# Two 16-head attentions: softmax sums written spread over the channels and inverted 512 wide, the spreading products removed, the key projection moved to the query's PSUM bank

## The reference

```python
q = (query @ Wq + bq).reshape(B, Nq, H, D).transpose(0, 2, 1, 3)      # H = 16 heads of D = 16
k = (key_value @ Wk + bk).reshape(B, Nkv, H, D).transpose(0, 2, 1, 3)
v = (key_value @ Wv + bv).reshape(B, Nkv, H, D).transpose(0, 2, 1, 3)
attn = jnp.einsum('bqhd,bhkd->bhqk', q, k) * scale
attn = jnp.clip(attn, -CLAMP, CLAMP)
attn = jax.nn.softmax(attn, axis=-1)
x = jnp.einsum('bhqk,bhkd->bqhd', attn, v).reshape(B, Nq, Cq)
return x @ Wo + bo
```

## Time and profile before

| | |
|---|---|
| median of 3 runs | 5029.59 us (5027.15 to 5030.32) |
| the profiled execution | 5077.9 us, span 5076.2 us |
| busy in the span | PE 4603.2 us (91%), DVE 3162.8 us (62%), ACT 1994.3 us (39%), POOL 1814.7 us (36%) |
| a0, first to last reciprocal | 70.3 to 597.4 us |
| a2, first to last reciprocal | 2164.4 to 2682.5 us |

### The profile page before, as it was taken

How to read it: one execution, slowest core, us unless ns; L and a number is a source line. 1 busy time by engine, 2 the same in 40 slices (tenths; PEclk the granted TensorE clock), 3 DMA queues, 4 the chain that set the end, 5 groups by cost and what they waited for, 6 DMA issues and landing times. The chain is left out here.

```text
span 5076.2 us, 91866 instructions
## 1 busy us (share of the span) xinstructions
PE 4603.2 (91%) x32540; PEld 3590.0 (71%) x32540; DVE 3162.8 (62%) x9688; ACT 1994.3 (39%) x4150; POOL 1814.7 (36%) x2248
## 2 busy tenths in 40 slices
PE   7999689988996999699996999999999967999979
PEld 5666457777775888566665888888888844777856
DVE  6888699965553331277773777777777743444344
ACT  3555367743442332245442333333333322222234
POOL 2222145532453331344530233333333312555532
PEclk9999899988997999799998999999999979999989
DMA  4666412144313222222212111111100055222233
GB/s 117 150 158 150 121 51 70 60 150 133 51 55 66 70 69 69 60 72 65 70 45 76 30 31 31 31 31 30 31 31 29 22 172 174 90 89 92 77 103 109
DMA packets 329713, 397.17 MB, mean 78 GB/s; under 512 B 66021, under 2 KB 289994, under 8 KB 318506
## 3 DMA queue, kind: packets, MB, share of 16 engines
q1 hardware_dynamic: 315946, 366.04, 25.5%
q0 software_dynamic: 13312, 25.25, 2.1%
HBM read 297.64 MB, written 93.55 MB: 77 GB/s over the span
## 5 line engine op out<-in xcount | busy, mean ns | idle before, releaser
L2540 PE MATMUL fa_h<-fa_xnT,fa_w 128*128 128x256 f32 x2048 | 485.6, 383 | 0.0
L2552 PE MATMUL fa_y<-fa_w,fa_hT 128*128 128x256 f32 x2048 | 462.5, 379 | 0.0
L2540 PEld LDWEIGHTS fa_h<-fa_xnT,fa_w 128*128 128x128 f32 x2048 | 382.5, 191 | 71.2 <-issue 13.2
L2552 PEld LDWEIGHTS fa_y<-fa_w,fa_hT 128*128 128x128 f32 x2048 | 386.8, 190 | 65.0 <-issue 14.8
L2419 ACT ACTIVATE fa_hT<-fa_h,fa_b 128x256 f32<-128x256 f32 x512 | 215.0, 471 | 544.2 <-PE fa_h L2540 482.3
L425 DVE TENSOR_REDUCE a_mx<-a_score 128x16 f32<-128x1920 f32 x128 | 275.9, 2156 | 83.8 <-PE a_score L609 74.6
L2926 ACT ACTIVATE m_hT<-m_h,m_b 128x256 f32<-128x256 f32 x256 | 107.5, 471 | 403.8 <-PE m_h L2963 403.8
L1566 PE MATMUL r_h<-r_xnT,r_rw 128*128 128x256 f32 x1024 | 251.2, 395 | 12.4 <-ACT r_hT L1524 11.5
L1867 ACT ACTIVATE e_hT<-e_h,e_b 128x256 f32<-128x256 f32 x256 | 107.5, 471 | 335.6 <-PE e_h L1921 327.6
L1706 POOL DMA_INDIRECT e_xg<-moe_rows,e_idx x64 | 128.6, 2009 | 308.5 <-issue 262.4
L1921 PE MATMUL e_h<-e_xT,e_w 128*128 128x256 f32 x1024 | 234.2, 382 | 2.5 <-DVE e_xT L1720 2.5
(11 more groups left out here) (453 smaller groups left out, 11009.6 us busy)
## 6 DMA issues: line engine op xcount, KB each, us to landing
a_floor<-a_lowest SPq DMA_DIRECT2D x64, 960.0 KB, 6.8
cv_toep<-kernels SPq DMA_DIRECT2D x16, 2048.0 KB
x<-a_xo SPq DMA_DIRECT2D x96, 256.0 KB, 4.1
f_xb<-x SPq DMA_DIRECT2D x64, 256.0 KB, 3.0
f_xres<-x SPq DMA_DIRECT2D x64, 256.0 KB, 3.0
a_xb<-x SPq DMA_DIRECT2D x64, 256.0 KB, 2.8
e_w<-in_L_ffn_ew SPq DMA_DIRECT2D x16, 1024.0 KB, 7.6
a_cb<-in_ctx SPq DMA_DIRECT2D x96, 90.0 KB, 2.3
```

Of the source, the lines that this page charges most:

```text
L2540: last = pe.matmul(h_ps[j % 2][:, c, :], w1[:, e, k, f:f + P], xnT[it.p][:, k, :], start=k == 0, stop=k == KD - 1)
L2552: last = pe.matmul(bank[:, t * D:(t + 1) * D], hT[e % 2][:, k, t * P:(t + 1) * P], w2[:, e, k, :], start=k == 0, stop=k == KE - 1)
```

## The change

`onesel` becomes two matrices of 32 columns, one for the even and one for the odd heads, with ones in 16 adjacent columns; a sum thus comes out of the same number of products on all 16 channels of its head. The two halves `m` no longer accumulate into one block of 256 columns, each has its own, so `total` is full with 512 columns. `reciprocals` becomes `invert`, 512 columns wide, and `weigh` becomes `divide`, which multiplies `raw` by `rec` itself; on DVE `divide` stands directly behind `invert`, ahead of `clips(0)` or `combine`. `widen`, its semaphore and `spread` are gone. `project_k` has no room in `total` any more: it goes to the right half of `front`, which it may write only when `q_out` has read the query from it (`q_ready`), and it stands behind `scores(1)`; `k_out` waits for `project_v` as well, and in a0 stands behind `exps(0)`.

```diff
-            def reciprocals(it):
+            def invert(it):
                 dve.wait_ge(av_ps, KD * it.i + 2)
-                if it.reused(1):
-                    dve.wait_ge(wide_ps, it.i)
-                dve.reciprocal(rec[:], total[:, 0:S]).then_inc(rec_ready, 1)
-
-            def weigh(it):
-                dve.wait_ge(wide_ps, it.i + 1)
+                dve.reciprocal(rec[:], by_k(total[:])).then_inc(rec_ready, 1)
+
+            def divide(it):
+                dve.wait_ge(rec_ready, it.i + 1)
                 dve.wait_ge(raw_ready, it.i + 1)
                 if it.reused():
                     dve.wait_ge(y_ps, it.i - 1)
-                dve.tensor_tensor(oT[it.p][:], raw[:], by_k(back[:]), ALU.mult).then_inc(oT_ready, 1)
+                dve.tensor_tensor(oT[it.p][:], raw[:], rec[:], ALU.mult).then_inc(oT_ready, 1)
...
-                    (3, maxima(0)), (5, reciprocals), (4, clips(0)), (1, norm_stats), (3, maxima(1)), (1, norm), (5, weigh),
+                    (3, maxima(0)), (5, invert), (5, divide), (4, clips(0)), (1, norm_stats), (3, maxima(1)), (1, norm),
...
             def k_out(it):
                 act.wait_ge(k_ps, it.i + 1)
+                act.wait_ge(v_ps, it.i + 1)
...
             def project_k(it):
                 pe.wait_ge(c_in[it.at], 16 * (it.round + 1))
-                if it.reused(1):
-                    pe.wait_ge(k_ready, 2 * it.i)
-                if it.reused(3):
-                    pe.wait_ge(rec_ready, it.i - 2)
+                pe.wait_ge(q_ready, it.i + 1)
                 for m in range(KD):
                     for k in range(2):
-                        last = pe.matmul(total[:, S + m * SK:S + (m + 1) * SK], wk[:, k, m * P:(m + 1) * P], cb[it.at][:, k, :],
+                        last = pe.matmul(front[:, S + m * SK:S + (m + 1) * SK], wk[:, k, m * P:(m + 1) * P], cb[it.at][:, k, :],
                                          start=k == 0, stop=k == 1)
...
                         for g in range(G):
-                            last = pe.matmul(total[g * 32:(g + 1) * 32, 0:S], onesel[:, m * E + e, :], pT[m][:, g, h * S:(h + 1) * S],
-                                             start=m == 0 and h == 0, stop=m == KD - 1 and h == E - 1)
+                            last = pe.matmul(total[g * 32:(g + 1) * 32, m * S:(m + 1) * S], onesel[:, e, :], pT[m][:, g, h * S:(h + 1) * S],
+                                             start=h == 0, stop=h == E - 1)
                     last.then_inc(av_ps, 1)
                 return step
-
-            def widen(it):
-                pe.wait_ge(rec_ready, it.i + 1)
-                if it.reused(1):
-                    pe.wait_ge(y_ready, it.i)
-                for m in range(KD):
-                    last = pe.matmul(back[:, m * S:(m + 1) * S], spread[:, m, :], rec[:], start=True, stop=True)
-                last.then_inc(wide_ps, 1)
```

More of the change, by code:

```diff
@@ L256, in heads_attention @@
                             "v_ready", "kd_ready"))
-    s_ps, maxed, mT_ps, taken, st_ps, exp_ready, av_ps, raw_ready, rec_ready, wide_ps, oT_ready, y_ps, y_ready = (
-        st.sem(n) for n in ("s_ps", "maxed", "mT_ps", "taken", "st_ps", "exp_ready", "av_ps", "raw_ready", "rec_ready",
-                            "wide_ps", "oT_ready", "y_ps", "y_ready"))
+    s_ps, maxed, mT_ps, taken, st_ps, exp_ready, av_ps, raw_ready, rec_ready, oT_ready, y_ps, y_ready = (
+        st.sem(n) for n in ("s_ps", "maxed", "mT_ps", "taken", "st_ps", "exp_ready", "av_ps", "raw_ready", "rec_ready", "oT_ready",
+                             "y_ps", "y_ready"))
     res_ready, bias_in, bias_ps, bias_ready = (st.sem(n) for n in ("res_ready", "bias_in", "bias_ps", "bias_ready"))
     NW = 8
-    MADE = 1 + 4 + 4 + SETS + KD + (1 if clip else 0)
+    MADE = 1 + 4 + 4 + E + (1 if clip else 0)
     MASKS = 9
@@ L320, in _ @@
             pool.wait_ge(made, 9)
-            one4 = onesel[:].rearrange("p j (a r) -> p j a r", r=SETS)
-            for j in range(SETS):
-                pool.memset(one4[:, j, :, j], 1.0).then_inc(made, 1)
-            for m in range(KD):
[L325 to L328, removed]
+            for e in range(E):
+                pool.memset(onesel[:, e, e * DH:(e + 1) * DH], 1.0).then_inc(made, 1)
             if clip:
@@ L472, in _ @@
                 pipeline(dve, B, DEPTH, [
-                    (3, maxima(0)), (5, reciprocals), (4, clips(0)), (1, norm_stats), (3, maxima(1)), (1, norm), (5, weigh),
+                    (3, maxima(0)), (5, invert), (5, divide), (4, clips(0)), (1, norm_stats), (3, maxima(1)), (1, norm),
                     (4, clips(1)), (3, put_max), (5, y_out)], **RUN)
             else:
-                pipeline(dve, B, DEPTH, later([(4, put_max), (3, maxima(0)), (5, reciprocals)]) + ([(2, combine)] if routed else []) + later([
-                    (1, norm_stats), (3, maxima(1)), (5, weigh), (1, norm), (5, y_out)]), **RUN)
+                pipeline(dve, B, DEPTH, later([(4, put_max), (3, maxima(0)), (5, invert), (5, divide)]) + ([(2, combine)] if routed else []) + later([
+                    (1, norm_stats), (3, maxima(1)), (1, norm), (5, y_out)]), **RUN)
         @block.scalar
@@ L506, in k_out @@
                 for m in range(KD):
[L507 removed]
+                    act.activation(kT[it.p][:, m, :], front[:, S + m * SK:S + (m + 1) * SK], ACT.Identity,
                                    bias=bk[:, m:m + 1]).then_inc(k_ready, 1)
@@ L544, in _ @@
                 pipeline(act, B, DEPTH, [
-                    (2, xT_out), (5, raw_out), (2, q_out), (2, k_out), (4, exps(0)), (2, v_out), (3, low_out), (4, exps(1))], **RUN)
+                    (2, xT_out), (5, raw_out), (2, q_out), (4, exps(0)), (2, k_out), (2, v_out), (3, low_out), (4, exps(1))], **RUN)
             else:
@@ L684, in _ @@
                 pipeline(pe, B, DEPTH, [
-                    (2, turn_x), (3, scores(0)), (5, attend(0)), (5, attend(1)), (4, shifted_scores(0)), (2, project_q), (2, project_k),
-                    (3, scores(1)), (5, widen), (2, project_v), (3, turn_max), (4, shifted_scores(1)), (5, project_o)], **RUN)
+                    (2, turn_x), (3, scores(0)), (5, attend(0)), (5, attend(1)), (4, shifted_scores(0)), (2, project_q),
+                    (3, scores(1)), (2, project_k), (2, project_v), (3, turn_max), (4, shifted_scores(1)), (5, project_o)], **RUN)
             else:
                 pipeline(pe, B, DEPTH, later([
-                    (2, turn_x), (3, scores(0)), (5, attend(0)), (5, attend(1)), (4, shifted_scores(0)), (2, project_q), (2, project_k),
-                    (3, scores(1)), (5, widen), (2, project_v), (4, shifted_scores(1)), (5, project_o), (3, turn_max)]), **RUN)
+                    (2, turn_x), (3, scores(0)), (5, attend(0)), (5, attend(1)), (4, shifted_scores(0)), (2, project_q),
+                    (3, scores(1)), (2, project_k), (2, project_v), (4, shifted_scores(1)), (5, project_o), (3, turn_max)]), **RUN)
     st.end()
```

13 lines of the change are left out of this document (6 added, 7 removed).

## The result

The changed kernel takes 5300.42 us (median of 4 runs, 5296.01 to 5303.56), the kernel before 5028.37 us in the same rounds: ratio 1.0539, 95% interval 1.0524 to 1.0554. It is 272 us slower where 161 were forecast. The direction held; the size lies outside the range of 5150 to 5250.

The account below looks back on a forecast made before the run. Neither PE nor DVE fills its stage; a ring of waits, mostly DVE's, sets the pace. Rings 128 us plus a0's clock 33 us make 161 us: 5190.6 us, 3.2% slower, range 5150 to 5250 us.

Parts of the forecast that it names:

- The rings: DVE's closed chain of waits per slot: longer by 2.32 us in a0, 1.95 us in a2; 70 and 58 us.
- The rival with the clock up: PE's clock stays at full speed, leaving only the 128 us of DVE terms: 5158 us, chance 0.22.
- The clock: PE's clock falls in a0 after 3.35 us idle before `scores(1)`: 1.1 us per slot, 33 us.
- I expect no fall there: In a2 the new PE gaps are shorter, so no clock fall; if it falls, 51 us.
- the sum: Whole kernel: 128 us of DVE terms plus 33 us of clock, 161 us, giving 5190.6 us.
- my upper bound of 2.9: Highest clock price per a0 slot, if `turn_max` and `shifted_scores(1)` double and projections outgrow `maxima(1)`: about 2.9 us.
- The rival "clock falls in both": PE's clock falls in a0 and a2, adding 51 us: 5242 us, chance 0.20.
- The key projection: Moved behind `scores(1)`: no change in a0; in a2 it waits for `q_out`, and `y_out` is just not held up.
- POOL's chain: In a2, POOL's work behind `k_out` up to `xres` ends at 11.8 us, before `y_out` at 12.19 us.
- the 48.3 us: Profiled execution of the kernel before stands this far above the median 5029.6 us; the difference carries over.
- the increment in a2: From the reciprocal, `maxima(1)` can start at 6.88 in place of 4.93 us: +1.95 us per slot.
- the slot of 19.05 us: Predicted length of a slot of a2 after the change, named among the signs to look for.

Follow-up runs that it names:

- the filled kernel: Changed kernel plus products nobody reads in PE's idle gaps, six in a0 and five in a2 per slot: 5165.37 us, ratio 1.0270.
- the narrow kernel: Changed kernel inverting only the first 256 columns, used for both halves, so half of the output's sums are wrong: 5141.93 us, ratio 1.0225.
- the reciprocal twice: Kernel before with one more reciprocal of 256 columns into a spare buffer ahead of its own in each slot: 5126.61 us, ratio 1.0183.
- the late product: Changed kernel with `divide` put where `weigh` was, behind the norm in a0 and behind `maxima(1)` in a2: 5213.88 us, ratio 1.0356.
- narrow kernel with the clock held: Changed kernel inverting only 256 columns, plus three products nobody reads in PE's gap in a0 and three in a2: 5069.92 us, ratio 1.0086.

## Why the prediction was right in direction and wrong in size

**The rings: right.** The reciprocal took 3358 ns (3374 forecast), the first clip followed it after 4.00 us (4.00), and the rings grew by 70.6 and 55.2 us (70 and 58), as the filled kernel shows. In its a2 `y_out` came 12.17 us after the reciprocal in one slot and 12.52 in another (12.19). The rival with the clock up gave 5158 us; the filled kernel took 5165, of which 8 are the later start.

**The clock: the step that failed, twice.** "I take 1.1 us, because the one short stretch at half speed ended after 3.41 us and the projections lie under cover" priced it at 33 us in a0, and "I expect no fall there" put none in a2. The runs give 67 us in a0 (61 by the stage's length) and 68 in a2, of the 135 us between the changed and the filled kernel. With the 8 us of a later start, which the sum had at nothing, that is the gap between 161 and 272 us: 34 + 68 + 8 = 110.

*The price.* The earlier trace rows held two stretches at 0.50, of 3.41 and of 10.24 us; I took the short one. In the slot of the changed kernel shown above it is 6.7 us with PE busy all the time, and the mean of 0.84 says much the same: (1 - 0.84) / 0.5 = 32% of 21.6 us is 6.9 us. In such a stretch it is not `scores(1)` that costs most; it can still run at full speed. The cost is the passage over key, value, `turn_max` and `shifted_scores(1)` to the second clip: 2.28 us a slot, near my upper bound of 2.9.

*The fall in a2.* In its slots PE stood idle 1.62 us before the key projection and, after the two projections, 0.89 us before `shifted_scores(1)`; the key projection ran at full clock (1.12 us), and the fall came near 2580.0, 1.5 us after the first gap's end, during the value projection. The gap of 0.89 us came behind the fall, so it can't have brought it on in this slot; and in the narrow kernel three products in the first gap alone kept a2 at 1.00. From 2580.60 to 2587.10 the clock was 0.52, the output projection took 3.45 in place of 1.99 us, and `y_out` waited 3.40 us for it (1.4 to 1.8 in the filled kernel). The gaps were near what I had worked out (1.5 and 1.2 us); what I took from their shortness was wrong. The rival "clock falls in both", 0.20, had the mechanism, with 5242 us; with the measured prices it is 5028 + 8 + 126 + 135 = 5297.

The Trainium skill, "TensorE: Matmul & The Clock Gate", section "Why this matters for your kernels", says that gaps between bursts of matmuls bring the clock back to half speed. This trace agrees for a0, where the gap was 3.41 us. The section speaks of longer gaps than a2's of 1.62 us; that such a gap is followed by the fall too stands on this case's traces alone.

**What brings the fall.** It does not need the width: with 256 columns the clock still fell (0.95 and 0.88). The key's place alone does not bring it: there it stayed at 0.99 and 1.00. Nor does a longer DVE arm alone, or hardly: with the reciprocal twice it stayed at 0.97 and 0.99. Two runs side by side show this best. From the reciprocal to a0's first clip, the kernel with the reciprocal twice takes 3.29 us and the changed kernel with the late product 3.28 us, so DVE's arm is the same; they differ in where PE's key projection stands and in whether it has the spreading products. With the key projection ahead of `scores(1)` and the spreading products behind it the clock fell in 4 of 29 slots of a0 and none of a2 (5126.61 us), without them in 24 and 21 (5213.88 us). The clock fell often only where the key projection and the spreading products had both left the stretch around `scores(1)` and DVE's arm was longer, by the product, by the width or by both. The departure of the two without a longer arm was not run on its own, so whether it would be enough stays open.

**The key projection: a term too low.** I cost it at nothing once POOL's chain fitted. POOL's chain did fit (`y_out` waited for PE). But the first reciprocal comes at 73.6 to 77.3 us in the eight kernels that have this key projection and invert on DVE, and at 68.2 to 70.4 in the others: 6.8 us of start-up between the medians. In the first 78 us of the kernel with the key projection alone moved, PE's key or value projection waits 6.1 us in all for `q_out`, against 2.7 us in the repeat of the kernel before, and from 50 to 60 us its clock is 0.50 against 0.86. How the 6.8 us divide between the two was not tested.

**The base.** Carrying the 48.3 us over was harmless but not for the reason given: they were no constant offset. Of the 39 us between the spans of the two executions (5076.2 and 5036.8) 23 were a2's slots (518.1 against 495.3) and 17 the routing and expert stages between a0 and a2 (1567.0 against 1549.7 us). It did not touch the terms, since the increment in a2 (+1.95 forecast, 18.08 - 16.21 = +1.87 measured) came from the rows at its ring. But the slot of 19.05 us that I named for a2 started from the odd 17.10; it measured 20.48 us, and 18.08 with the clock held.

**The parts, as measured.** The narrow kernel with the clock held is 44 us over the kernel before (product's place, key projection), the width adds 95, the clock 135: 5026 + 44 + 95 + 135 = 5300. These are differences along one row of runs, so they close whatever the cause; that each is what its name says rests on the edits and the slots above.

## What to carry to other kernels

Where an edit lengthens the arm on which TensorE waits and at the same time takes small products out of that wait, price the clock over everything that TensorE does in the next stretch at half speed, not over the one operation behind the gap, and look for gaps of one or two microseconds too (1.62 us here). Test it with products that nobody reads: if the kernel gets faster with more work, it was the clock. And read a base trace from two executions where its own time stands 1% above the median.

An operation that seems idle weight on the busiest engine (256 instructions less for PE here) may be what fills a wait, while one microsecond on the engine that closes the ring is paid in every slot.

## What the runs showed of the hardware

- A reciprocal of the sums out of PSUM took 958 ns for 128 columns, 1758 for 256 and 3358 for 512: 6.25 ns a column on top of 158 ns. The line that I had drawn through the 2 columns of another tile (154 ns, 6.31 ns a column) was slightly too steep; the line through these three would have 170 ns for 2 columns.
- `pow` on GpSimd took 41.3 us for 256 columns of 128 channels, and 0.72 us for 2 columns (to the power -0.5, in the norm); it is no way to move an inversion of this size.
- In the first execution of the kernel before, a2's slots were 0.88 us longer at the same clock, throughout the stage, with PE's weight loads idle for 0.86 us of it; the repeat did not show it. The cause is open.
